# Gathered rows turned by DMA transposes from a two-part fp16 store, in place of TensorE transposes

## The reference

```python
mod = (silu(c) @ wmod)                     # sa, ca, ga, sb, cb, gb for each batch; ga, gb kept away from 0
h = layernorm(x) * (1 + ca) + sa
x = x + ga * attn(h)                       # 16 heads of 16; only the 409 queries of largest norm per head attend
h = layernorm(x) * (1 + cb) + sb
# mixture of experts: E = 8, F = 1024, the two best experts of each token
probs = softmax(h @ router_w + router_b)
topk_w, topk_i = top_k(probs, 2); topk_w = topk_w / sum(topk_w)
y_e = relu(h @ w1[e] + b1[e]) @ w2[e] + b2[e]
x = x + gb * sum over the two experts of topk_w * y_e
```

## Time and profile before

| | us |
|---|---|
| runs (median of 3; lowest to highest) | 1340.1 (1339.38 to 1342.72) |
| the profiled execution | 1339.05 |
| its span | 1337.3 |
| TensorE, VectorE busy | 1056.1, 971.2 |
| ScalarE, GpSimd busy | 614.7, 621.5 |
| routing tiles, first to last L1288 | 691.0 to 791.1 |
| expert stage, first to last matmul of the hidden layer | 864.3 to 1300.2 |

### The profile page before, as it was taken

How to read it: one execution, slowest core, us unless ns; L and a number is a source line. 1 busy time by engine, 2 the same in 40 slices (tenths; PEclk the granted TensorE clock), 3 DMA queues, 4 the chain that set the end, 5 groups by cost and what they waited for, 6 DMA issues and landing times. The chain is left out here.

```text
span 1337.3 us, 29836 instructions
## 1 busy us (share of the span) xinstructions
PE 1056.1 (79%) x7678; PEld 653.4 (49%) x7679; DVE 971.2 (73%) x2481; ACT 614.7 (46%) x1367; POOL 621.5 (46%) x648
## 2 busy tenths in 40 slices
PE   7997101399999999999736672499999999999991
PEld 4443101133333333333225550188888888888881
DVE  3766579888888888888338877667777777777770
ACT  2777000067777777777525540044444444444440
POOL 0688300444555555553328981134444444545531
PEclk9999555589999999999869875599999999999996
DMA  6244500211111111111079970012232323222325
GB/s 204 99 162 145 210 0 0 53 28 34 44 42 37 34 42 42 34 38 28 4 234 305 314 237 1 24 28 46 47 47 47 47 47 47 47 47 47 47 33 141
DMA packets 84803, 104.17 MB, mean 78 GB/s; under 512 B 17040, under 2 KB 72016, under 8 KB 84496
## 3 DMA queue, kind: packets, MB, share of 16 engines
q1 hardware_dynamic: 61616, 77.32, 18.4%
q0 software_dynamic: 21632, 23.11, 10.9%
q10 hardware_dynamic: 1504, 3.15, 0.7%
HBM read 63.30 MB, written 44.42 MB: 81 GB/s over the span
## 5 line engine op out<-in xcount | busy, mean ns | idle before, releaser
L846 DVE TENSOR_REDUCE attend_mxh<-attend_p_a 128x1 f32<-128x512 f32 x416 | 263.5, 684 | 50.3 <-PE attend_p_a L981 45.9
L920 ACT ACTIVATE attend_prob<-attend_p_b 128x409 f32<-128x409 f32 x480 | 231.7, 515 | 99.8 <-PE attend_p_b L997 94.9
L1641 ACT ACTIVATE expert_hr<-expert_p,b1t 128x256 f32<-128x256 f32 x312 | 131.0, 471 | 224.8 <-PE expert_p L1592 224.8
L1553 POOL DMA_INDIRECT acc_d<-expert_ys,expert_drop x78 | 129.8, 1665 | 208.1 <-DVE expert_ys L1673 180.1
L1606 PE MATMUL expert_p<-w,expert_hhi 128*128 x1248 | 213.9, 273 | 5.8 <-DVE expert_hlo L1698 4.6
L1592 PE MATMUL expert_p<-expert_xhi,w 128*128 128x256 f16 x1248 | 214.6, 275 | 3.6 <-DVE expert_xlo L1681 1.5
L1606 PE MATMUL expert_p<-w,expert_hlo 128*128 x624 | 170.1, 273 | 0.0
L997 PE MATMUL attend_p_b<-attend_qt,attend_kt 99*128 99x409 bf16 x480 | 164.2, 346 | 0.3 <-ACT attend_prob L920 0.3
L801 POOL DMA_INDIRECT attn_d<-attend_outs,idx x96 | 93.8, 977 | 145.9 <-DVE attend_otail L874 126.4
L981 PE MATMUL attend_p_a<-attend_kt,attend_qt 96*128 96x512 bf16 x384 | 151.0, 397 | 7.2 <-DVE attend_mxh L846 4.9
L1606 PEld LDWEIGHTS expert_p<-w,expert_hhi 128*128 128x128 f16 x1248 | 121.9, 98 | 29.3 <-issue 12.5
(11 more groups left out here) (299 smaller groups left out, 1717.4 us busy)
## 6 DMA issues: line engine op xcount, KB each, us to landing
route_wraw<-in_L_ffn_w SPq DMA_DIRECT2D x32, 512.0 KB, 5.5
q_d<-project_q SPq DMA_DIRECT2D x32, 256.0 KB, 2.1
k_d<-project_k SPq DMA_DIRECT2D x48, 128.0 KB
attend_kt<-k_d SPq DMA_DIRECT2D x32, 192.0 KB, 2.9
x<-in_L_attn_x SPq DMA_DIRECT2D x8, 512.0 KB, 10.6
attn_d<-zero SPq DMA_DIRECT2D x8, 512.0 KB, 5.7
attend_kt<-k_d SPq DMA_DIRECT2D x32, 128.0 KB, 3.0
route_ain<-attn_d SPq DMA_DIRECT2D x32, 128.0 KB, 4.9
```

The lines of the kernel that those rows point to most:

```text
L846: dve.tensor_reduce(mxh[:, c, k:k + 1], chunk_bank(a)[:, :], AX, ALU.max).then_inc(a_done, 1)
L920: act.activation(prob[:, j, :], tile_bank(j)[:, 0:TOP], ACT.Exp, scale=SCALE).then_inc(prob_done, 1)
L1553: pool.indirect_dma_start(out=io["acc_d"], out_offset=bass.IndirectOffsetOnAxis(ap=drop[u][:, s:s + 1], axis=0), in_=ys[u][:, s, :], in_of ...
L1641: act.activation(hr[g % 2][:, f, :], p_1[g][:, f, :], ACT.Relu, bias=cst["b1t"][:, bass.ds(e * FB + 2 * g + f, 1)], scale=1.0 / WSCALE).th ...
```

## The change

In the routing tiles ScalarE copies each tile of h to fp16 (`high_part`, ahead of `copy_h`), VectorE subtracts this from h and writes the rest as fp16 (`rest_part`, ahead of `add_rb`). SP stores the two parts side by side in the 256 words that held h as fp32. In the expert block SP gets a list: for each tile it waits for the gathered rows and for the hidden layer two tiles back, and issues two DMA transposes from `xs` to `xt`, each of 128 rows by 512 fp16 values. `turn`, `high`, `low` and `p_x` are gone. TensorE waits for the transposes at g = 0, and GpSimd's gather for those of the tile that had the buffer.

```diff
@@ route_block
+        h16 = [sb(f"h16{i}", [P, 2, D], F16) for i in range(4)]
+        hi_done, lo_done = sem("hi_done"), sem("lo_done")
...
                 def save_h(t, c):
-                    sp.wait_ge(h2_done, t + 1)
-                    sp.dma_start(h2v[bass.ds(t, 1)].rearrange("a p d -> (a p) d"), h2[c][:, :]).then_inc(h2_saved[c], 16)
+                    sp.wait_ge(lo_done, t + 1)
+                    sp.dma_start(h2v[bass.ds(t, 1)].rearrange("a p d -> (a p) d"), h16[c][:, :, :].rearrange("p a d -> p (a d)").bitcast(I32)).then_inc(h2_saved[c], 16)
...
+                def high_part(t, c):
+                    act.wait_ge(h2_done, t + 1)
+                    wait(act, h2_saved[c], 16 * (t // 4))
+                    act.activation(h16[c][:, 0, :], h2[c][:, :], ACT.Copy).then_inc(hi_done, 1)
+
                 def copy_h(t, c):
+                    high_part(t, c)
...
                 def modulate(t, c):
-                    wait(pool, h2_saved[c], 16 * (t // 4))
+                    wait(pool, lo_done, t - 3)
...
+                def rest_part(t, c):
+                    dve.wait_ge(hi_done, t + 1)
+                    dve.tensor_tensor(h16[c][:, 1, :], h2[c][:, :], h16[c][:, 0, :], ALU.subtract).then_inc(lo_done, 1)
...
-                pipeline(dve, [None, cut, residual, normal, None, None, None, add_rb])
+                pipeline(dve, [None, cut, residual, normal, None, None, rest_part, add_rb])
@@ expert_block
+            @block.sync
+            def _(sp):
+                def turn(j, u):
+                    sp.wait_ge(x_here[u], 16 * SUB * ((j - u) // 2 + 1))
+                    sp.sem_inc(x_turn, 1)
+                    wait(sp, h_ps, G * (j - 1))
+                    sp.sem_inc(x_turn, 1)
+                    for s in range(SUB):
+                        sp.dma_start_transpose(xt[u][:, :, :, s * P:(s + 1) * P].rearrange("p a k n -> p (a k) n"), xs[u][:, s, 0:D].bitcast(F16)).then_inc(xt_here[u], 16)
...
                 def gather(j, u):
-                    wait(pool, x_ps, j - 1)
+                    wait(pool, xt_here[u], 16 * SUB * ((j - u) // 2))
...
                     if g == 0:
-                        pe.wait_ge(xlo_done, j + 1)
+                        pe.wait_ge(xt_here[u], 16 * SUB * ((j - u) // 2 + 1))
...
-                                last = pe.matmul(p_1[g][:, f, :], w, xp[u][:, k, :], start=(n == 0), stop=(n == 3 * KD - 1))
+                                last = pe.matmul(p_1[g][:, f, :], w, xt[u][:, xpart, k, :], start=(n == 0), stop=(n == 3 * KD - 1))
...
                 def gates(j, u):
-                    dve.wait_ge(xlo_done, j + 1)
+                    dve.wait_ge(x_here[u], 16 * SUB * ((j - u) // 2 + 1))
```

More of the change, by code:

```diff
@@ L1374, in _ @@
                     with nc.allow_non_contiguous_dma(reason="two gates for each row"):
-                        sp.dma_start(io["h2_d"].rearrange("(t p) w -> p t w", p=P)[:, :, D:HW], gate[:, :, :]).then_inc(gate_saved, 16)
+                        sp.dma_start(io["h2_d"].rearrange("(t p) w -> p t w", p=P)[:, :, D:HW], gate[:, :, :].bitcast(I32)).then_inc(gate_saved, 16)
                     sp.wait_ge(gate_saved, 16)
@@ L1492, in expert_block @@
         XB = 2
-        xs = [sb(f"xs{i}", [P, SUB, HW], F32) for i in range(XB)]
-        xhi = [sb(f"xhi{i}", [P, KD, MT], F16) for i in range(2)]
-        xlo = [sb(f"xlo{i}", [P, KD, MT], F16) for i in range(2)]
+        xs = [sb(f"xs{i}", [P, SUB, HW], I32) for i in range(XB)]
+        xt = [sb(f"xt{i}", [P, 2, KD, MT], F16) for i in range(2)]
         hr = [sb(f"hr{i}", [P, 2, MT], F32) for i in range(2)]
@@ L1507, in expert_block @@
         x_here, y_saved = [sem(f"x_here{i}") for i in range(XB)], [sem(f"y_saved{i}") for i in range(2)]
-        x_ps, xhi_done, xlo_done, h_ps, relu_done, hhi_done, hlo_done, y_ps, y_done = (
-            sem("x_ps"), sem("xhi_done"), sem("xlo_done"), sem("h_ps"), sem("relu_done"), sem("hhi_done"), sem("hlo_done"), sem("y_ps"), sem("y_done"))
+        xt_here, x_turn = [sem(f"xt_here{i}") for i in range(2)], sem("x_turn")
+        h_ps, relu_done, hhi_done, hlo_done, y_ps, y_done = (
+            sem("h_ps"), sem("relu_done"), sem("hhi_done"), sem("hlo_done"), sem("y_ps"), sem("y_done"))
         G = FB // 2
@@ L1535, in expert_block @@
         with nc.Block() as block:
+            @block.sync
[7 more added lines that the diff above has]
+                        sp.dma_start_transpose(xt[u][:, :, :, s * P:(s + 1) * P].rearrange("p a k n -> p (a k) n"), xs[u][:, s, 0:D].bitcast(F16)).then_inc(xt_here[u], 16)
+                steps(sp, turn)
             @block.gpsimd
@@ L1588, in hidden @@
                         n = 0
-                        for part, xp in ((0, xhi), (0, xlo), (1, xhi)):
+                        for part, xpart in ((0, 0), (0, 1), (1, 0)):
                             for k in range(KD):
                                 w = cst["w1"][:, bass.ds(e, 1), k, part, c0:c0 + P].rearrange("p a f -> p (a f)")
-                                last = pe.matmul(p_1[g][:, f, :], w, xp[u][:, k, :], start=(n == 0), stop=(n == 3 * KD - 1))
+                                last = pe.matmul(p_1[g][:, f, :], w, xt[u][:, xpart, k, :], start=(n == 0), stop=(n == 3 * KD - 1))
                                 n += 1
@@ L1619, in body @@
                             output(j - 1, 1 - u, g, before)
-                        if g == 1 and has(j + 1):
-                            turn(j + 1, 1 - u)
                 steps(pe, body)
@@ L1629, in _ @@
             def _(act):
[L1630 to L1633, removed]
                 def body(j, u):
@@ L1642, in body @@
                                            scale=1.0 / WSCALE).then_inc(relu_done, 1)
-                        if g == 1 and has(j + 1):
-                            high(j + 1, 1 - u)
                         if has(j - 1) and g < SUB:
@@ L1677, in rows_of @@
                     dve.tensor_copy(take[u][:, :], cst["take"][:, bass.ds(SUB * j, SUB)]).then_inc(take_done, 1)
-                def low(j, u):
-                    dve.wait_ge(xhi_done, j + 1)
-                    dve.tensor_tensor(xlo[u][:, :, :], p_x[:, :, :], xhi[u][:, :, :], ALU.subtract).then_inc(xlo_done, 1)
                 def gates(j, u):
-                    dve.wait_ge(xlo_done, j + 1)
-                    dve.tensor_tensor(both[u][:, :, :], xs[u][:, :, D:HW], cst["pick"][:, bass.ds(SUB * j, SUB), :], ALU.mult).then_inc(both_done, 1)
+                    dve.wait_ge(x_here[u], 16 * SUB * ((j - u) // 2 + 1))
+                    dve.tensor_tensor(both[u][:, :, :], xs[u][:, :, D:HW].bitcast(F32), cst["pick"][:, bass.ds(SUB * j, SUB), :], ALU.mult).then_inc(both_done, 1)
                     dve.wait_ge(both_done, j + 1)
@@ L1698, in body @@
                         dve.tensor_tensor(hlo[u][:, 2 * g:2 * g + 2, :], hr[g % 2][:, :, :], hhi[u][:, 2 * g:2 * g + 2, :], ALU.subtract).then_inc(hlo_done, 1)
-                        if g == 1 and has(j + 1):
-                            low(j + 1, 1 - u)
                         if has(j - 1) and g >= 2:
@@ L1707, in _ @@
                 rows_of(1, 1)
-                low(0, 0)
                 gates(0, 0)
```

5 lines of the change are left out of this document (1 added, 4 removed).

## The result

The changed kernel takes 1343.86 us in the median of 19 runs (1341.63 to 1348.1), the kernel before 1338.88 in 19 (1335.61 to 1343.21). The ratio is 1.0037 [1.0029, 1.0046]: slower by 5.0 us, where 1339, half a microsecond less than before, was forecast.

What follows compares the result with a forecast made beforehand. TensorE was taken to bound the expert stage, VectorE and GpSimd together the routing tiles, DMA close behind. Expert -12.9 (-16.3 + 2.4 + 1.0) and routing +12.4 gave -0.5 us: 1339, range 1328 to 1385.

Steps and rivals of the forecast that it cites:

- SP's new wait: Routing tiles: SP's store waits for VectorE's subtraction, so the next tile's loads go out later; no further loss was forecast.
- L_w: Routing tiles: time from the weights' issue to their landing; 4.6 us allowed, trace median 5.5, least 3.7.
- rival 3: Routing tiles: loads come late; with weights landing in 5.5 us the stage costs +21.4 us, total 1348; chance 0.12.
- 3T >= 6.5 + L_w: Routing tiles: three steps must cover 6.5 us plus the weights' landing time; a 3.71 us step allows 4.6.
- The subtraction: Routing tiles: VectorE's added instruction costs 0.40 us per tile over 31 steps, +12.4 us (10.2 to 15.5).
- Rival 4: Routing tiles: the subtraction costs nothing, since a phase shift gives L1288 its 1.20 us back; total 1327; chance 0.10.
- The copy: Routing tiles: ScalarE's fp16 copy, about 0.36 us per tile, is covered by its wait for the weights; no cost.
- GpSimd's wait for the subtraction: Routing tiles: GpSimd's `modulate` waits for the subtraction four tiles back, done a step before it is needed; no cost.
- TensorE's transposes: Expert stage: removing four transposes per tile shortens the step from 11.28 to 10.85 us, 16.3 us gained.
- L and the start: Expert stage: rows' arrival to landing of both DMA transposes takes 5 us, delaying the first hidden matmul by 2.4.
- Rival 2: Expert stage: DMA transposes outlast their 10.0 us and TensorE waits in each body; total 1385 to 1407; chance 0.28.
- The cold clock: Start of the expert stage: matmuls, no longer the transposes, take TensorE's slow time; 1.0 us lost, at most 1.3.

## Why the prediction was wrong

The step that failed is the one that priced SP's new wait at nothing: "At T = 3.71 this allows L_w = 4.6 ... I take no further loss, and keep 5.5 as a rival". The wait is not free: it cost 7.1 and 7.3 us in the two pairs that isolate it. This is rival 3's mechanism at a smaller L_w than its 5.5. The condition, 3T >= 6.5 + L_w, named it: the weights landed in 5.0 us in the median, so T = (6.5 + 5.0) / 3 = 3.83, and 3.82 was measured. That it meets the number so closely is in part luck. In the step shown the weights leave 5.59 us after its start (740.54), not 5.35, since the subtraction took 0.95; the kernel with split and wait should have 3.80 (L_w = 4.9) and has 3.75; and with the weights first the condition allows 3.5 and the step was 3.90. So it gives the loss by the late weights and not the trade with GpSimd, whose x comes late too. Two things went wrong in it. I had a row that broke the condition, a median of 5.5, and argued it away with emptier DMA engines: they were emptier (96% to 86% busy), and the landing was 0.5 us shorter where 0.9 was needed. And I took the 3.31 of one tile for the step, where the mean was 3.23: with that T is 3.63 (the kernel with the later store has 3.61), the condition allows 4.4, and the loss is 31 x (3.82 - 3.63) = 5.9 us of steps. The forecast's own sign of being wrong, a step beyond 3.9, did not catch it, and that 1344 lies inside its own range of 1334 to 1348 is luck: this range was for L and for the size of the subtraction.

The other steps:

- **The subtraction, forecast +12.4.** Measured +14.0 for the whole kernel alone, of which 10.6 in the 31 steps, and 9.9 in the steps of the pair without the late store. The mechanism is right, and the size within its bounds of 10.2 to 15.5 in one of the two readings and just below in the other. VectorE's 0.41 turns to 0.95 when it starts under GpSimd's L1269, but this is traded against L1296, which then starts clear of GpSimd (1.23 where L1288 took 1.57). I had read in the earlier trace rows that L1288 and L1253 slow each other. The rows say something narrower, shown in the last section: L1253 waits for L1288, and L1288 for GpSimd's L1261 before it.
- **Rival 4, the subtraction for nothing through a shift in phase.** Refuted: the shift happened (L1296 from a median of 1492 ns to 1226) and the subtraction took its place beside GpSimd. In the two kernels without the wait L1296 kept its length (medians 1580 and 1666) and the subtraction cost 10 us all the same.
- **The copy, forecast 0.** Right: 100.0 against 100.1 us.
- **GpSimd's wait for the subtraction, forecast 0.** In the changed kernel none shows. With the store out of the way it is 7.5 and 8.7 us in all (9 and 12 times), of unknown price.
- **TensorE's transposes, forecast -16.3.** Right: first to last is 17.9 shorter, with no wait in steady state. About 1 of the other 1.6 is the clock, below.
- **L and the start, forecast L = 5 and +2.4.** Measured 4.1 and +1.5. Whether it was the idle DMA engines, as I argued, no run shows. The Trainium skill, "Advanced Engine Details and Errata", section X-Bar Transpose, says that such transposes are as fast as regular DMAs; the trace agrees (4.1 against 2.9 for the gather and SP's second issue). "VectorE: DVE Perf Modes", section The three transpose paths, gives 1309 ns for a 128 x 128 block by DMA; the two transposes, eight such blocks, did not take the 10.5 us estimated from it, and the measured 4.1 decides.
- **Rival 2, the transposes outlast 10 us.** It did not happen: twice as many were still free. With six spare ones it does happen, and by the formula 1408 was expected where 1418.87 was measured: it has the waits (38 x 1.48 = 56, measured 52.9) and not the lower clock that came with them.
- **The cold clock, forecast +1.0.** Wrong in sign. Three stretches of the changed kernel, then two of the kernel before, with the granted clock as the third number from the end:

```profile
887.00:889.00 2.00, 2.00 (x12) 1.39 (x11) 0.00 (x0) 0.00 (x0) 1.38 (x2) 0.50 0.45 102
889.00:891.00 2.00, 2.00 (x14) 1.56 (x13) 0.53 (x2) 0.84 (x2) 0.51 (x1) 0.66 0.44 128
891.00:893.00 2.00, 2.00 (x21) 1.79 (x19) 1.30 (x3) 1.15 (x3) 0.00 (x0) 1.00 0.04 8
```

```profile
864.00:870.00 6.00, 5.73 (x28) 4.35 (x28) 1.62 (x6) 1.14 (x3) 1.89 (x2) 0.50 0.16 44
870.00:872.00 2.00, 2.00 (x20) 1.79 (x20) 1.39 (x3) 1.30 (x4) 0.00 (x0) 1.00 0.03 8
```

The lower level (0.50, 1.2 GHz) now lasts from 886.67 to about 890.4 (a mean of 0.66 over two microseconds is 1.36 of them at 0.50), 3.7 us; it lasted from 864.27 to 870, 5.7 us. Half of the difference, 1 us, is gained where I put 1.0 lost. What made it shorter is not shown; TensorE ran without a hole in the one (2.00 of 2.00) and not in the other (5.73 of 6.00).

- **The sum.** The expert stage was forecast at -12.9 and gave -17.9 + 1.5 + 1.3 = -15.1. Up to its first gather +12.4 was forecast and +20.9 came. The two misses, -2.2 and +8.5, make the 6.3 us between the forecast's -0.5 and the +5.8 of the spans. For the kernel with the later store (1336.6) the forecast of 1339 holds to 3 us.

## What to carry to other kernels

A store that waits for late work holds back every load queued behind it on the same engine: put one step later in the pipeline, it gave some 7 us back here. Where a condition in your working fails with the value that a row shows, let it fail, and do not argue the row down to the value that saves it. Work that can go to either of two stages belongs in the one where its engine has idle time: the same copy and subtraction cost 10 us in routing, where VectorE was full, and 3 us in the expert stage (421.4 from first to last matmul, against 418.4 in the kernel without the subtraction). The best kernel with the split in routing took 1336.6, the best with the split in the expert stage 1328.8.

## What the runs showed of the hardware

- A DMA transpose of 128 x 512 two-byte values keeps SP 1.25 us, where a plain issue records 0.35:

```profile
L1557 SPq DMA_TRANSPOSE expert_xt<-expert_xs x78: 1189/1253/1332, 882.6 to 1288.7; - x78
```

- In the routing tiles a VectorE instruction with two inputs in SBUF and a GpSimd instruction beside it do not each slow down: the one that starts later waits for the other to end. The subtraction of 0.41 us takes 0.95 under GpSimd's L1269, and in the two steps shown it ends 0.28 us after L1269 does (744.28 after 744.00, 748.34 after 748.07), while L1269 keeps nearly its shortest time (0.78 and 0.82; 0.72 at the least). The kernel before does the same ahead of the rows:

```profile
744.29 0.79 POOL L1261 TENSOR_TENSOR route_h<-route_xn,mod 128x256 f32<-128x256 f32 x1 [0.19 <-POOL route_xn L1260]
```

L1288 starts under it (744.59) and ends 1.08 us after it; L1253 starts under L1288 (745.04) and ends 0.59 after that. Each time it is the instruction's own shortest time less some 0.13 us. From 722 to 792 us of that trace L1288 starts 21 times under L1261 and ends 1.07 to 1.09 after it in 20 of them (1.15 in the other), and L1253 ends 0.58 to 0.60 after L1288 in 21 of 21. The Trainium skill, "SBUF — State Buffer", section SBUF: two separate sides, states it so: a VectorE instruction with two SBUF inputs and a GpSimd instruction that reads SBUF take the shared ports as a lock, and the later one blocks. The trace agrees.
